# Decoder layer on one core: output projection and normalisations spread over the slots, the rotation's products all on VectorE

## What is computed

```python
x = x + attn(layernorm(x))       # 32 heads of 64, 8 key/value heads, causal window of 128, a sink per head
x = x + xattn(ctx, ctx, layernorm(x))   # a long convolution per channel, then a product with the query
x = x + ffn(layernorm(x))        # sum of 8 factors, one 512 x 512 matrix
```

```python
qkv = x @ qkv_w.T + qkv_b
q = rope(q); k = rope(k)         # concat(x1 * cos - x2 * sin, x2 * cos + x1 * sin)
logits = q @ k / 8, masked;  m = max(logits)
w = exp(logits - m) / (sum(exp(logits - m)) + exp(sink - m))
out = (w @ v) @ out_w.T + out_b
```

## Time and profile before

| | |
|---|---|
| median of 3 runs | 2186.37 us (2185.14 to 2190.4) |
| the profiled execution | 2186.3 us, span 2184.5 us |
| busy, share of the span | PE 1989.6 (91%), DVE 1614.5 (74%), ACT 935.3 (43%), POOL 767.7 (35%) |
| L641 exps, ACT | x1024, 391 ns each |
| L628 bent, ACT | x320, 470 ns each, 134.1 us |
| L712 products, POOL | x160, 1293 ns each, 206.9 us |
| L845 den, DVE | x256, idle before it 346.5 us, of it 316.2 for ACT's es L644 |
| mean granted TensorE clock | 0.974 of full |

### The profile page before, as it was taken

One profiled execution on the slowest core, in us unless ns is written; L12 is line 12 of the kernel. 1 busy time (PEld: TensorE's weight loads), 2 busy tenths in 40 slices (PEclk: granted clock), 3 DMA queues, 4 the chain that ended last, 5 costly groups with the idle time before them and its releaser, 6 DMA issues. The chain is left out here.

```text
span 2184.5 us, 48974 instructions
## 1 busy us (share of the span) xinstructions
PE 1989.6 (91%) x15488; PEld 1614.8 (74%) x15488; DVE 1614.5 (74%) x5784; ACT 935.3 (43%) x3481; POOL 767.7 (35%) x879
## 2 busy tenths in 40 slices
PE   5799999899999988989999999999996899999699
PEld 4577777777777777778878777878874577677587
DVE  4777767676767767677777676777774699999787
ACT  3444444444444444445444454545442222222233
POOL 2234333333333323322333223232330454454354
PEclk8999999999999999999999999999998899999799
DMA  5136211111111122111211111111101633333364
GB/s 185 51 88 143 72 50 50 50 59 50 50 50 55 53 88 68 40 59 51 86 51 49 51 50 50 59 51 50 64 35 66 226 91 86 84 89 87 106 226 157
DMA packets 73984, 170.67 MB, mean 78 GB/s; under 512 B 6928, under 2 KB 15632, under 8 KB 73632
## 3 DMA queue, kind: packets, MB, share of 16 engines
q1 hardware_dynamic: 64160, 146.80, 20.2%
q0 software_dynamic: 3840, 8.39, 2.1%
q10 hardware_dynamic: 5760, 12.59, 1.5%
HBM read 109.03 MB, written 50.41 MB: 73 GB/s over the span
## 5 line engine op out<-in xcount | busy, mean ns | idle before, releaser
L641 ACT ACTIVATE pr<-pr,mx 128x128 f32<-128x128 f32 x1024 | 399.0, 391 | 470.5 <-DVE mx L836 470.5
L712 POOL TENSOR_TENSOR m<-m,rope_sb 128x512 f32<-128x512 f32 x160 | 206.9, 1293 | 542.8 <-ACT m L628 542.8
L501 PE MATMUL wP<-xTh,wh 128*128 128x256 f32 x1280 | 380.8, 298 | 9.3 <-DVE m L812 4.9
L501 PE MATMUL wP<-xTl,wh 128*128 128x256 f32 x1280 | 366.3, 286 | 0.0
L501 PE MATMUL wP<-xTh,wl 128*128 128x256 f32 x1280 | 365.2, 285 | 0.0
L1067 PE MATMUL y<-kv,tap 128*128 128x288 f32 x1280 | 329.2, 413 | 27.7 <-DVE res L1115 9.7
L1067 PEld LDWEIGHTS y<-kv,tap 128*128 128x128 f32 x1280 | 239.9, 191 | 116.9 <-issue 25.9
L845 DVE TENSOR_TENSOR den<-ac,es 128x4 f32<-128x4 f32 x256 | 61.5, 240 | 346.5 <-ACT es L644 316.2
L562 PE MATMUL oP<-woh,oTh 128*128 128x512 f32 x512 | 230.1, 449 | 48.2 <-DVE x L884 48.2
L501 PEld LDWEIGHTS wP<-xTh,wh 128*128 128x128 f32 x1280 | 248.7, 194 | 14.5 <-issue 5.7
L501 PEld LDWEIGHTS wP<-xTl,wh 128*128 128x128 f32 x1280 | 249.0, 195 | 0.0
(11 more groups left out here) (108 smaller groups left out, 3790.2 us busy)
## 6 DMA issues: line engine op xcount, KB each, us to landing
tap<-padded_taps SPq DMA_DIRECT2D x64, 256.0 KB, 3.4
kk<-in_ctxt SPq DMA_DIRECT2D x64, 192.0 KB, 3.1
x_in<-in_x SPq DMA_DIRECT2D x16, 512.0 KB, 4.0
xt_split<-xTh SPq DMA_DIRECT2D x16, 512.0 KB, 3.8
xt_split<-xTl SPq DMA_DIRECT2D x16, 512.0 KB, 5.1
xb<-in_x SPq DMA_DIRECT2D x16, 512.0 KB, 4.6
fsum<-in_factors POOLq DMA_DIRECT2D x8, 1024.0 KB, 8.5
x_part_rows<-x SPq DMA_DIRECT2D x16, 512.0 KB, 3.1
```

Of the source, the lines that this page charges most:

```text
L501: last = pe.matmul(wP[:, h * T:(h + 1) * T], w[:, n, c, h * P:(h + 1) * P], a[:, s, c, :], start=(c == 0 and i == 0), stop=(c == KD - 1 an ...
L641: act.activation(pr[:, s, a, cols], pr[:, s, a, cols], ACT.Exp, bias=mx[:, s, i:i + 1], scale=-1.0, accum_out=ac[:, s, i:i + 1])
L712: pool.tensor_tensor(m2[:, s], m2[:, s], rope_sb[:, 1 if i == 0 else 0, 1:3], ALU.mult).then_inc(sin_ready, 1)
```

## The change

It has three parts.

1. **Rotation.** `bent` and GpSimd's product are gone. `turned` on VectorE does four scalar_tensor_tensors out of `wP` instead of two: bias added, times cosine into `m1`, times minus sine or sine into the swapped halves of `m2`. It waits for the unit itself (`qk_done`). GpSimd's `rotate` keeps the sum.
2. **Output projection.** The parts stand in slots by a table: part 1 in slot 1, 2 and 3 in slot 2, 4 in slot 3, 5 and 6 in slot 4, 7 in slot 5, 0 in slot 7, and none in slots 0 and 6. Before, slot s had part s + 1.
3. **Normalisations.** They are cut into tiles. First layernorm (sweep 0): stats after the mask of slots 4 and 6, for two windows ahead, the end in slots 0 and 1, one tile each. Second (sweep 1): stats in slot 4 and in the next window's slot 0, the end in slots 1 and 2. GpSimd's `power` now stands behind `sinks_shifted`, in slot 6 for the first and in slot 0 for the second.

```diff
+        RESIDUAL_AT = {3: 0, 7: 1}
+        PARTS_AT = {1: [1], 2: [2, 3], 3: [4], 4: [5, 6], 5: [7], 7: [0]}
...
+        def parts_of(y, p, j):
             sl = 2 * (p % 4) + j
-            return None if y.first or sl not in (3, 7) else sl // 4
+            if y.first and p < 7 or y.drain and p == 7 and j == 1:
+                return []
+            return PARTS_AT.get(sl, [])
...
-                        if out_here(y, p, j):
-                            out_projection(y, p, j)
+                        for s in parts_of(y, p, j):
+                            out_projection(y, p, s)
...
-            def bent(y, p, i):
-                v = y.window(p)
-                s = (p // 4 + i) % 2
-                act.wait_ge(qk_done, (QM + 1) * v + i + 1)
-                wait(act, qr_ready, (QM + 1) * v + i - 1)
-                for half in range(2):
-                    last = act.activation(m2[:, s, 1 - half], wP[:, half * T:(half + 1) * T], ACT.Identity,
-                                          bias=bqk_sb[:, y.sweep, i, half:half + 1])
-                last.then_inc(bent_ready, 1)
...
-                pool.tensor_tensor(m2[:, s], m2[:, s], rope_sb[:, 1 if i == 0 else 0, 1:3], ALU.mult).then_inc(sin_ready, 1)
-                pool.wait_ge(sin_ready, (QM + 1) * v + i + 1)
                 pool.wait_ge(m_ready, (QM + 1) * v + i + 1)
...
-                        if p % 4 == 0 and j == 0 and fresh(y, p):
-                            power(veps, rstd, ve_ready, rstd_ready, y.window(p) + 2)
-                        if residual_tile(y, p, j) == 1 and late(y, 2, p):
-                            power(ve2, rs2, ve2_ready, rs2_ready, y.window(p) - 2 - B + 1)
                         if y.here(p, 2):
...
                             sinks_shifted(y, p, j)
...
+                        if p % 4 == 3 and j == 0 and x_after(y, p):
+                            power(veps, rstd, ve_ready, rstd_ready, y.window(p) + 3)
+                        if p % 4 == 0 and j == 0 and late(y, 3, p):
+                            power(ve2, rs2, ve2_ready, rs2_ready, y.window(p) - 3 - B + 1)
...
-                wait_apart(dve, passed, (bent_ready, (QM + 1) * v + i + 1), (qr_ready, (QM + 1) * v + i - 1))
-                for half in range(2):
-                    last = dve.scalar_tensor_tensor(m1[:, s, half], wP[:, half * T:(half + 1) * T], bias[:, half:half + 1],
-                                                    tab[:, 0], ALU.add, ALU.mult)
+                wait_apart(dve, passed, (qk_done, (QM + 1) * v + i + 1), (qr_ready, (QM + 1) * v + i - 1))
+                for dst, h, half, f in [(m1, 0, 0, 0), (m1, 1, 1, 0), (m2, 0, 1, 1), (m2, 1, 0, 2)]:
+                    last = dve.scalar_tensor_tensor(dst[:, s, h], wP[:, half * T:(half + 1) * T], bias[:, half:half + 1],
+                                                    tab[:, f], ALU.add, ALU.mult)
                 last.then_inc(m_ready, 1)
...
-                if old and t == NT - 1:
-                    dve.wait_ge(x1_ready, 2 * r + 2)
-                    layernorm_start(x1, st2, mv2, ve2, ln2_chain, 2 * (r - B), ve2_ready)
...
+                        sl = 2 * (p % 4) + j
+                        if sl in (4, 6) and x_after(y, p):
+                            ln1_stats(y.window(p) + 2, (sl - 4) // 2)
...
+                        elif sl in (0, 1) and fresh(y, p):
+                            ln1_end(y.window(p) + 1, sl)
+                        if sl == 4 and late(y, 2, p):
+                            ln2_stats(y.window(p) - 2, 0)
+                        if sl == 0 and late(y, 3, p):
+                            ln2_stats(y.window(p) - 3, 1)
+                        if sl in (1, 2) and late(y, 3, p):
+                            ln2_end(y.window(p) - 3, sl - 1)
```

More of the change, by code:

```diff
@@ L260, in fresh, with x_after @@
             return y.sweep == 0 and not (y.number == HM - 1 and p >= 4)
+        def x_after(y, p):
+            return y.sweep == 0 and y.number != HM - 1
         def x_next(y, p, j):
@@ L564, in out_projection @@
                 last.then_inc(out_done, 1)
-            def out_here(y, p, j):
-                last_slot = p % 4 == 3 and j == 1
-                if y.first:
-                    return p == 7 and j == 1
-                return not (y.drain and p == 7 and j == 1)
             for t in range(NT):
@@ L675, in body @@
                             p_evac(y, p, j)
-                        n = unit_of(p, j)
-                        if n is not None and n != V_UNIT and not y.drain:
-                            bent(y, p, rope_index(n))
                         if x_next(y, p, j):
@@ L763, in _ @@
             bodies(pool, body)
+            power(ve2, rs2, ve2_ready, rs2_ready, B)
             pool.wait_ge(f_in, 16 * RANK)
@@ L767, in _, with layernorm_stats, layernorm_spread @@
         def _(dve):
-            def layernorm_start(src, st, mvv, ve, chain, n, ready):
-                for t in range(NT):
-                    last = dve.bn_stats(st[:, t, :], src[:, t, :])
-                last.then_inc(chain, 1)
-                wait_apart(dve, passed, (chain, n + 1))
+            def layernorm_stats(src, st, t, chain):
+                dve.bn_stats(st[:, t, :], src[:, t, :]).then_inc(chain, 1)
+            def layernorm_spread(st, mvv, ve, chain, n, ready):
+                wait_apart(dve, passed, (chain, 3 * n + 2))
                 for t in range(NT):
@@ L884, in residual, with ln2_stats, ln2_end @@
                 dve.tensor_tensor(x1[:, t, :], oP[:], xb[:, t, :], ALU.add).then_inc(x1_ready, 1)
-                if old and t == NT - 1:
-                    dve.wait_ge(x1_ready, 2 * r + 2)
-                    layernorm_start(x1, st2, mv2, ve2, ln2_chain, 2 * (r - B), ve2_ready)
-            def ln2_end(r):
+            def ln2_stats(r, t):
+                dve.wait_ge(x1_ready, 2 * r + t + 1)
+                layernorm_stats(x1, st2, t, ln2_chain)
+                if t == NT - 1:
+                    layernorm_spread(st2, mv2, ve2, ln2_chain, r - B, ve2_ready)
+            def ln2_end(r, t):
                 dve.wait_ge(rs2_ready, r - B + 1)
-                wait(dve, x1t_done, 2 * (r - B))
-                layernorm_end(x1n, x1, mv2, rs2, x1n_ready)
+                wait(dve, x1t_done, 2 * (r - B) - 1 + t)
+                layernorm_end(x1n, x1, mv2, rs2, x1n_ready, t)
             dve.wait_ge(mhalf_set, 1)
-            ln1_start(0)
-            ln1_end(0)
+            for t in range(NT):
+                ln1_stats(0, t)
+            for t in range(NT):
+                ln1_end(0, t)
             split_low(0, 0)
@@ L927, in body @@
                             o_low(y, u, jj)
-                        if p % 4 == 0 and fresh(y, p):
-                            if j == 0:
-                                ln1_start(y.window(p) + 1)
-                            else:
-                                ln1_end(y.window(p) + 1)
-                        if p % 4 == 0 and j == 0 and late(y, 3, p):
-                            ln2_end(y.window(p) - 3)
+                        sl = 2 * (p % 4) + j
+                        if sl in (4, 6) and x_after(y, p):
+                            ln1_stats(y.window(p) + 2, (sl - 4) // 2)
+                        if y.first and p == 0:
+                            for t in range(NT):
+                                if j == 0:
+                                    ln1_stats(1, t)
+                                else:
+                                    ln1_end(1, t)
+                        elif sl in (0, 1) and fresh(y, p):
[6 more added lines that the diff above has]
+                            ln2_end(y.window(p) - 3, sl - 1)
                         for i, n in split_now(y, p, j):
@@ L937, in _ @@
             bodies(dve, body)
-            ln2_end(2 * B - 1)
+            ln2_stats(2 * B - 1, 1)
+            for t in range(NT):
+                ln2_end(2 * B - 1, t)
 def conv_part(nc, ctx_in, pad_dram, q2_dram, big):
```

36 lines of the change are left out of this document (17 added, 19 removed).

## The result

The changed kernel takes 2245.04 us (median of 4 runs, 2237.74 to 2247.77), the kernel before, run beside it, 2185.76 (4 runs): a ratio of 1.0257, 95% interval 1.0239 to 1.0274. It is slower by 59 us. The forecast was 2276 us in a range of 2215 to 2295, so side and range hold, and the size is 31 us too high. The profiled execution is the fastest of the four (2237.74 us, +51.4 against the 2186.3 of before).

The account below looks back on a forecast made before the run. VectorE's closed loop with ScalarE, at least 4.87 us per slot plus work ahead of the mask, was taken as the bound. Sweep 0 +25.7, sweep 1 +56.4, jumps +4, edges +4: together +90, 2276 us, range 2215 to 2295.

Parts of the forecast that it names:

- The queue price of the products: VectorE, ahead of the mask: two more products per rotation at 0.395 us each, +3.95 us per window, under no cover.
- Sweep 0: Windows of sweep 0: +3.95 - 1.52 - 0.9 = +1.53 us each, plus 0.45 for power over den.
- 1.52 of power ahead of sk: Sweep 0, slot 0: GpSimd's power ahead of sk delayed den by 1.52 us; moved behind sk, this loss goes.
- waits for bent: VectorE's products waiting for ScalarE's bent: 0.9 us per window in sweep 0 and 1.4 in sweep 1, to go completely.
- Item 1: Slot 6 of sweep 0 and slot 0 of sweep 1: GpSimd's power holds den, 0.45 us (bounds 0 and 0.48).
- Item 2: Sweep 1, slot 2: TensorE's chain behind the later normalised tile 0 delays the products of slot 3, +1.3 us.
- Item 3: Sweep 1, slot 4: TensorE from slot 3's unit to slot 5's takes 11.95 us against VectorE's 11.32, +0.65.
- Item 4: Sweep 1, before the transposes of Item 2: TensorE idles about 3 us, the clock drops, 1.6 us lost (bounds 0 and 1.6).
- Jumps and edges: Sweep 1's four jumps, no longer absorbing a wait: +4 us; first window and those around the change of weights: +4.
- no drop of the clock: Rival: Item 4 at 0, as the idle is shorter or does not bring it; +70, 2256 us, chance 0.25.
- Only VectorE's queue counts: Rival: the new chains have slack and power does not hold den; +29, 2215 us, chance 0.12.
- the extra products lie beside something: Faster rival: two extra products cost under 0.3 us per slot instead of 0.79; -46, 2140 us, chance 0.07.

Follow-up runs that it names:

- Single parts: The changed kernel with one part of the output projection in every slot, as before the change: 2211.13 us, ratio 1.0087 against the kernel before.
- the sums apart: GpSimd's two xb sums put in slots 2 and 3 instead of both in slot 2, on five kernels: 2158.16 to 2234.65 us.

## Why the prediction was right, and where its sizes were off

**The queue price of the products** was the main term, and it holds: 1.57 us for four in every rotation slot, nothing hidden. Undoing them alone gives back 59.3 us. That exchange also brings bent and GpSimd's product back, and a kernel with six products per rotation, planned to tell the queue from bent and the bank, gave no time. What shows the queue is the length of the slots: 6.43 = 4.87 + 1.57 in the changed kernel, where the shortest before was 5.65 = 4.87 + 0.79.

**Sweep 0** was forecast at +1.98 per window with the power's 0.45, or +1.53 without; it measured 50.70 - 49.12 = +1.58, and +1.49 as the mean of the eight windows that no jump touches. The 1.52 of power ahead of sk, the waits for bent and the unchanged 0.82 are thereby right as a sum. The 1.52 can be seen alone: from the mask of slot 0 to that of slot 1 it was 7.18 us before and 6.44 after, which is 0.79 more and 1.52 less.

**Item 1 is the step that was wrong.** The prediction took 0.45 "since power is the same kind of instruction". It ran over den in 27 windows, and den took 0.16 to 0.17 in each. That removes 26 x 0.45 = 12 us. The 128x512 sums do hold den (0.97). The power has two elements per partition, and why it does not hold den was only observed, not tried.

**Item 2** was right in place and size, 1.29 for 1.3. Moving the tile a slot earlier removed it.

**Item 3** was right in place, 0.45 for 0.65: it costs 13 x 0.2 = 3 us less than said. Single parts removed it as well.

**Item 4** had the right mechanism and too large a sum. The idle is 2.65 at most, not about 3 (the prediction's own terms, 9.2 - 5.7, even give 3.5), and the time lost where the clock fell is mostly the 1.4 to 1.6 that was said, but it fell in 6 of 13 windows. That is some 10 us in place of 20. When it falls is not settled: after 2.65 us of idle it did both. The profiled run had a mean clock of 0.969 and the other three 0.965 to 0.966, so those probably had more such windows; with the sums apart, a profile of the otherwise same kernel at 0.962 has 9 in the same 13.

**Jumps and edges** were forecast at +8. In the profiled run the sweep 0 jumps were cheaper than before by some 8 us: the slots that hold them took 8.1 to 10.3 where other slots take 6.44, and before 9.9 to 10.4 where others take 5.8. In other kernels with the same products single ones took 11.8 to 12.8, so this is not put down to the change: it is luck. In sweep 1 the jumps' +4 did not arrive: about 3 us of absorbed wait were indeed lost, and the slots with the jumps were as much cheaper. The edges gave -5.0 + 6.6 - 2.0 = -0.4.

So from +90: -12 (power), -3 (item 3), -10 (clock), and -8 (jumps and edges) give +57, and -8 more for this run's cheap jumps +49, where the profiled run has +51. The other three executions took 6 to 10 us more at a lower mean clock. They have no trace, so whether the clock or the jumps made that is not shown.

**Of the rivals**, "no drop of the clock" (2256) came nearest to the median, for a mixed reason: the clock did drop, less often, and the power cost nothing. "Only VectorE's queue counts" fell, since the chains of items 2 and 3 are there. That the extra products lie beside something fell too: den still waits up to 1.48 and no rotation slot is under 6.43. The rule of the Trainium skill named in the prediction (SBUF — State Buffer, "Who interferes with whom") would give item 1 its full 0.48, and the trace contradicts it for the power, at 0.16 in 27 of 27 meetings. The same section of the Trainium skill says that `tensor_scalar` can take the shared ports in a two-port mode; the trace agrees, 1.80 against 0.87 for four scalings under a GpSimd sum.

**What was not foreseen** is that the parts of the change lean on each other. Alone, the products cost 3.15%, the table 1.75% and the normalisations 0.5%; together they cost 2.57%. The table alone lengthens the idle ahead of the transposes, and the spread normalisations alone bring TensorE ahead of VectorE and GpSimd's product onto the scalings. The change with four products has no GpSimd product to collide, which is why single parts and spread normalisations cost 43.5 us for the products with the sums apart but only 9.5 with them together (2211.1 against 2201.6). Why TensorE falls into the pattern that waits 3.3 us when den is held, and not when it is free, was shown by taking the hold away but not followed step by step.

## What to carry to other kernels

When an engine's slot is a closed loop of a queue and a fixed wait, price an added instruction by its place in the slot, not by the engine's busy share: with VectorE at 77% busy every product ahead of the mask cost its full 0.39 us. Before work is moved into a wait, look at what the neighbouring engine starts there and which bank is freed later by it: one GpSimd sum of 1.29 us holds whichever instruction of den or the scalings meets it, and setting two such sums apart was worth 2% of the time in one kernel. Try the parts of a change together and singly: here each alone was a loss, and the normalisations alone, with the sums apart, a gain of 1.6%.

## What the runs showed of the hardware

- A GpSimd operation on 128x512 tiles holds one VectorE instruction by up to 1.1 us, and the held one may be a sum of 128x4 (1.14 for 0.16) or a scaling of 128x128 by a value per partition (four in 1.80 for 0.87). The mask's instructions and the products that read PSUM stood beside the same sums without being longer (0.42 and 0.48 us, with and without).
- A GpSimd power on 128x2 took 0.70 us and did not hold den, which began 0.20 into it, in 27 of 27 cases.
- After 2.46 to 2.65 us of idle the granted clock behind TensorE's next work fell to the lower level (1.2 GHz) in six windows and stayed at 2.4 GHz in four others of the same run. After 1.96 us it stayed in three of three.
- The slot with a loop jump took from 7.9 to 13.1 us in these kernels, where the same slot without one takes 5.6 to 7.8. It differs between the jumps of one run (8.1 to 10.3 in sweep 0 of the changed kernel) and between kernels with the same instructions in it.
